# Routing without a stage of its own: choices and ranks inside the neighbouring stages, one memory region per expert

## The reference

```
x = x + layernorm(attention(layernorm(x)))     # 16 heads of 16, prefix-LM mask, output projection + bias
x = x + layernorm(moe(layernorm(x)))

def moe(x):                                     # 8192 tokens
    scores = softmax(x @ gate_w.T)              # 8 experts
    idx    = top_k(scores + gate_b, 2)
    cw     = one_hot(idx) * scores, summed      # weights of the two chosen experts
    y_e    = swiglu((x@w1_e.T + b1_e) * (x@w3_e.T + b3_e)) @ w2_e.T + b2_e
    return sum_e cw_e * y_e + shared expert(x)  # same form, for all tokens
```

## Time and profile before

| | us |
|---|---|
| median of 3 runs (2283.53 to 2286.15) | 2284.32 |
| profiled execution, its own time | 2304.21 |
| its span, first to last instruction | 2302.5 |

### The profile page before, as it was taken

One profiled execution on the slowest core, in us unless ns is written; L12 is line 12 of the kernel. 1 busy time (PEld: TensorE's weight loads), 2 busy tenths in 40 slices (PEclk: granted clock), 3 DMA queues, 4 the chain that ended last, 5 costly groups with the idle time before them and its releaser, 6 DMA issues. The chain is left out here.

```text
span 2302.5 us, 38058 instructions
## 1 busy us (share of the span) xinstructions
PE 2083.7 (90%) x14085; PEld 1272.9 (55%) x14085; DVE 1465.9 (64%) x2297; ACT 1698.6 (74%) x2162; POOL 661.2 (29%) x643
## 2 busy tenths in 40 slices
PE   7995999999999999999997883799999999999970
PEld 6782333333333333333333883688888888888860
DVE  5663255554555565554555895465688888888865
ACT  5664999999999999999996771333466666666645
POOL 1111000000000000000000450766335665666537
PEclk9997999999999999999999995899999999999995
DMA  6887645565544445555501771544467776677656
GB/s 222 309 289 182 131 90 97 105 104 102 102 65 89 88 87 93 104 105 73 86 10 51 233 267 65 188 161 163 161 199 213 193 173 176 171 186 187 174 168 252
DMA packets 162899, 340.50 MB, mean 148 GB/s; under 512 B 18048, under 2 KB 91904, under 8 KB 155424
## 3 DMA queue, kind: packets, MB, share of 16 engines
q1 hardware_dynamic: 130148, 284.29, 46.4%
q0 software_dynamic: 30256, 46.03, 10.7%
q10 hardware_dynamic: 2316, 7.80, 0.9%
HBM read 194.29 MB, written 143.62 MB: 147 GB/s over the span
## 5 line engine op out<-in xcount | busy, mean ns | idle before, releaser
L1114 ACT ACTIVATE att_prob<-att_scores 128x1024 f32<-128x1024 f32 (+2 forms) x1122 | 998.0, 1031 | 61.5 <-PE att_scores L1061 58.1
L1080 PE MATMUL att_out<-att_prob,att_va 128*32 128x512 f32 (+3 forms) x5000 | 578.9, 543 | 13.6 <-DVE att_prob L1146 12.1
L1061 PE MATMUL att_scores<-att_qs,att_ks 50*128 50x512 f32 (+3 forms) x2560 | 466.5, 431 | 22.9 <-PEq L116 17.2
L1061 PEld LDWEIGHTS att_scores<-att_qs,att_ks 50*128 50x128 f32 x2560 | 211.3, 185 | 495.4 <-ACT att_prob L1114 415.4
L1782 POOL DMA_INDIRECT sums<-moe_y,moe_token x142 | 307.1, 2162 | 247.9 <-ACT moe_y L2040 194.1
L1924 PE MATMUL moe_ps<-moe_xt_hi,moe_w_hi 128*128 128x512 f32 (+1 forms) x880 | 340.2, 387 | 21.5 <-ACT moe_h L2013 17.2
L1009 POOL DMA_DIRECT2D ctx_scr<-att_cout x64 | 55.1, 861 | 985.2 <-DVE att_cout L1196 946.2
L1924 PE MATMUL moe_ps<-moe_xt_hi,moe_w_lo 128*128 128x512 f32 (+1 forms) x880 | 333.8, 379 | 0.0
L1924 PE MATMUL moe_ps<-moe_xt_lo,moe_w_hi 128*128 128x512 f32 (+1 forms) x880 | 332.5, 378 | 0.0
L1146 DVE SCALAR_TENSOR_TENSOR att_prob<-att_prob,att_tri 128x512 f32<-128x512 f32 x224 | 144.8, 688 | 271.3 <-ACT att_prob L1114 271.3
L2013 ACT ACTIVATE moe_h<-moe_ps,moe_wb 128x512 f32<-128x512 f32 (+1 forms) x220 | 141.6, 650 | 112.6 <-PE moe_ps L1924 57.0
(11 more groups left out here) (259 smaller groups left out, 3201.9 us busy)
## 6 DMA issues: line engine op xcount, KB each, us to landing
qk_parts<-proj_qk SPq DMA_DIRECT2D x64, 512.0 KB, 4.6
keep_first_weights<-w_experts SPq DMA_DIRECT2D x22, 1412.0 KB
moe_wraw<-w_experts SPq DMA_DIRECT2D x21, 1412.0 KB
att_qs<-qk_parts SPq DMA_DIRECT2D x180, 128.0 KB
att_ks<-qk_parts SPq DMA_DIRECT2D x180, 128.0 KB
rows_in<-att_zeros SPq DMA_DIRECT2D x13, 1632.0 KB, 21.7
moe_rows<-rows_in SPq DMA_DIRECT2D x22, 544.0 KB
proj_xin<-x SPq DMA_DIRECT2D x16, 512.0 KB, 3.8
```

Source lines behind the costliest of these rows:

```text
L1061: last = nc.tensor.matmul(pss[e % SBUFS][:, h, at:at + CH - q0], ks[s][rows, half, kt * P:(kt + 1) * P], qs[s][rows, half, c * CH + q0:(c ...
L1080: last = nc.tensor.matmul(pso[k % 2][strip, q0:], va[team % 2][:, kt, strip], probs_of(u)[:, h, at:at + CH - q0], start=(kt == 0), stop=(i ...
L1114: nc.scalar.activation(probs_of(u)[:, half * 2:half * 2 + 2, start:], pss[e % SBUFS][:, :, start:], ACT.Exp, scale=HD ** -0.5)\
```

## The change

There is no routing stage. Each expert has a region of its own in `rows_in`, of 8192 + 512 rows, so that a token's place is `8704 * expert + rank` and needs no total counts. The 64 tiles are worked in 4 groups of 16:

- End of the output stage: the maximum is subtracted from the logits of groups 0, 1, 2 in steps 9, 13, 17 (group 3 behind the last step), with ScalarE's exponentials behind them. In steps 17 to 20 VectorE also makes shares and scores (17) and choices (18) of group 0, shares and scores of group 1 (19), ranks of group 0 and choices of group 1 (20). TensorE has two counting matmuls in step 18. The shared expert's weights are loaded at step 2 and cut into hi and lo in steps 17 and 18; the first rows are loaded at step 6.
- Inside `experts`: TensorE counts groups 1, 2, 3 behind block 0 of chunks 0, 2, 4 into the PSUM of the second product; VectorE makes their ranks at f = 1 of these chunks, shares and scores of groups 2, 3 at f = 3 of chunks 0, 2, their choices at f = 1 of chunks 1, 3. The tables of chunks follow at f = 1 and f = 3 of chunks 5, 6, 7. POOL waits for the ranks of a group ahead of chunks 4, 8 and 12.
- Filling: the zero fills during attention are gone (two transfers of 512 rows stay, one into `blank`). SP copies `blank` (512 rows, 557 KB) behind every expert's last row, 8 copies from memory to memory, ahead of its load of chunk 10.
- SP reads the start of each routed chunk from a table and loads from there.

```diff
+REGION = T + CH
+SPARE_AT = E * REGION
...
 # attention_out, SP
+                    if k == 2:
+                        sp.dma_start(first_raw[:], w_experts[E]).then_inc(w_loaded[0], 16)
+                    if k == ADD + 3:
+                        sp.wait_ge(xn_stored[0], 16)
+                        sp.dma_start(first_rows[:, :, 0:D], tok_ch[0]).then_inc(rows_loaded[0], 16)
...
 # attention_out, TensorE (CHOOSE_AT = CUT_AT = NCH + 1)
+                    if k == CHOOSE_AT + 1:
+                        count_first()
...
 # attention_out, ScalarE, at the end of a step
+                    if k == CUT_AT:
+                        act.wait_ge(w_loaded[0], 16)
+                        nc.scalar.activation(w_first[0][:, 0:W13], first_raw[:, 0:W13], ACT.Copy).then_inc(w_hi[0], 1)
+                    if k == CUT_AT + 1:
+                        nc.scalar.activation(w_first[0][:, W13:], first_raw[:, W13:WM], ACT.Copy).then_inc(w_hi[0], 1)
+                        nc.scalar.activation(wb_first[:], first_raw[:, WM:], ACT.Copy).then_inc(w_bias[0], 1)
...
 # attention_out, VectorE: behind residual, add_bias and context_lo of a step
+                    if k == CHOOSE_AT:
+                        shares_of(V, r, group_tiles(0), then)
+                        scores_of(V, r, group_tiles(0), then)
+                    if k == CHOOSE_AT + 1:
+                        best_two_of(V, r, group_tiles(0), tails, then)
+                        dve.sem_inc(marked, 1)
+                    if k == CHOOSE_AT + 2:
+                        shares_of(V, r, group_tiles(1), then)
+                        scores_of(V, r, group_tiles(1), then)
+                    if k == CHOOSE_AT + 3:
+                        dve.wait_ge(counted, 2)
+                        ranks_of(V, dve, r, 0, counts[:, 0], counts[:, 1], slot, then, counts_read, 0)
+                        best_two_of(V, r, group_tiles(1), tails, then)
+                    if k == CUT_AT:
+                        dve.wait_ge(w_hi[0], 1)
+                        V.tensor_tensor(w_first[1][:, 0:W13], first_raw[:, 0:W13], w_first[0][:, 0:W13].bitcast(F32),
+                                        ALU.subtract).then_inc(w_lo[0], 1)
...
+                shift_logits(GROUPS - 1)
...
+def ranks_of(V, dve, r, g, before, total, slot, then, counts_read, seen):
+    V.tensor_copy(r.total, total.rearrange("p (t e) -> p e t", e=E)).then_inc(counts_read, 1)
+    then(V.tensor_tensor_scan(r.upto..., r.keeps..., r.total..., 0.0, ALU.mult, ALU.add))
+    then(V.tensor_tensor(r.at, ... upto - total))
+    V.tensor_tensor(r.at, r.at, before..., ALU.add).then_inc(counts_read, 1)
+    then(V.tensor_tensor(r.at, r.at, bcast(r.run[g], 1, [P, GT, E]), ALU.add))
+    then(V.tensor_tensor(r.run[g + 1], r.run[g], r.upto[:, :, GT - 1], ALU.add))
+    then(V.tensor_tensor(r.tmp, r.hot[:, :, t], ..., ALU.mult))
+    then(V.tensor_reduce(r.slotf, r.tmp, AX_X, ALU.add))
+    then(V.tensor_copy(slot[:, :, t], r.slotf))
...
 # experts, SP
+        COUNT_AT, TABLE_AT, FILL_AT = (0, 2, 4), 5, 10
+                    if c == FILL_AT:
+                        sp.wait_ge(fills_known, 1)
+                        for e in range(E):
+                            at = sp.value_load(fill_at[0:1, e:e + 1], min_val=0, max_val=SPARE_AT)
+                            sp.dma_start(rows_in[bass.ds(at, CH), :]..., blank...).then_inc(blanked, 16)
...
+                            if k == 0:
+                                sp.wait_ge(blanked, E * 16)
+                                sp.wait_ge(experts_known, 2)
+                            at = sp.value_load(start_of[0:1, region(k):region(k) + 1], min_val=0, max_val=SPARE_AT)
+                            sp.dma_start(ring[b][:, 0:held], rows_in[bass.ds(at, held * P), :]...)
...
 # experts, TensorE
-                    hidden(n, s, range(0, FB - 1))
+                    hidden(n, s, range(0, 1))
+                    if c in COUNT_AT:
+                        count(COUNT_AT.index(c) + 1, c)
+                    hidden(n, s, range(1, FB - 1))
+                    if c - 1 in COUNT_AT or c in COUNT_AT[1:]:
+                        pe.wait_ge(counts_read, 2 * sum(1 for a in COUNT_AT if a <= c))
                     if prv is not None:
                         down(*prv)
...
 # experts, ScalarE, ahead of the first rows
+                        nc.scalar.activation(r.ex[:, t], r.ex[:, t], ACT.Exp).then_inc(r_exped, 1)
                         rows(0, 0)
-                        second_weights(0, 0)
...
 # experts, VectorE, behind u of block f and ahead of the rest
+                        route(c, f)
+                def route(c, f):
+                    if f == 1 and c in COUNT_AT:
+                        ranks(COUNT_AT.index(c) + 1)
+                    for g in range(2, GROUPS):
+                        if (c, f) == (COUNT_AT[g - 1] - 2, 3):
+                            shares_of(...); scores_of(...)
+                        if (c, f) == (COUNT_AT[g - 1] - 1, 1):
+                            best_two_of(V, r, t, tails, then)
+                            dve.sem_inc(marked, 1)
+                    # (5,1) halves, (5,3) bases, (6,1) singles, (6,3) owners, (7,1) places, (7,3) chosen
```

More of the change, by code:

```diff
@@ L920, in attend @@
         ZR = 12
[L921 to L922 removed]
+        assert len({(ZR * p + j) % CH for p in range(P) for j in range(TPC)}) == CH
         SR = (T + CH - FIRST * CH) // P // 2
@@ L1353, in router, with count_first @@
                     last.then_inc(g_done, 1)
+                def count_first():
+                    pe.wait_ge(marked, 1)
+                    both = r.both[:, group_tiles(0)].rearrange("p t e -> p (t e)")
+                    for i, left in enumerate((r.before, r.onesq)):
+                        nc.tensor.matmul(counts[:, i], left, both, start=True, stop=True).then_inc(counted, 1)
                 for k in range(STEPS):
@@ L1653, in experts @@
         HALVED = (3, PAIRS - 1)
-        whole = {p: ph.sb(f"acc{p}", [P, 2, TPC, D])[:] for p in range(3)}
+        places = [late[:, i * 2 * TPC * D:(i + 1) * 2 * TPC * D].rearrange("p (c j d) -> p c j d", c=2, j=TPC)
+                  for i in range(3 + EARLY)]
+        whole = {p: places[p] for p in range(3)}
         whole.update({4 + i: chunks_in(wraw[i][:], 2) for i in range(2)})
@@ L1942, in down, with count @@
                         last.then_inc(y_done[s], 1)
+                def count(g, c):
+                    if g > 1:
+                        pe.wait_ge(marked, g - 1)
+                        pe.wait_ge(y_biased[c % 2], c // 2 * 2)
+                    both = r.both[:, group_tiles(g)].rearrange("p t e -> p (t e)")
+                    for left, psum in ((r.before, psY[0]), (r.onesq, psY[1])):
+                        nc.tensor.matmul(psum[:, 0, 0:GT * E], left, both, start=True, stop=True).then_inc(counted, 1)
                 def step(n, s, nxt, prv):
+                    c = 2 * n + s
                     if prv is None:
@@ new lines, in owners @@
+                def owners():
+                    starts = r.chunk0.unsqueeze(2).broadcast_to(slots)
+                    then(V.tensor_tensor(r.past[:, :, 1:], starts, bcast(r.ends, 1, slots), ALU.is_ge))
+                    then(V.tensor_tensor(r.alone, starts, bcast(r.single, 1, slots), ALU.is_equal))
+                    then(V.tensor_tensor(r.alone, r.alone, bcast(r.odd, 1, slots), ALU.mult))
+                    then(V.tensor_tensor(r.mine, r.past[:, :, 0:E], r.past[:, :, 1:], ALU.subtract))
+                    then(V.tensor_tensor(own[:], r.mine, r.alone, ALU.add))
@@ new lines, in places @@
+                def places():
+                    starts = r.chunk0[0:1].unsqueeze(2).broadcast_to(one)
+                    then(V.tensor_tensor(r.from_[0:1], starts, bcast(r.shift[0:1], 1, one), ALU.add))
+                    then(V.tensor_tensor(r.from_[0:1], r.from_[0:1], r.mine[0:1], ALU.mult))
+                    then(V.tensor_tensor(r.also[0:1], r.alone[0:1], bcast(r.single_at[0:1], 1, one), ALU.mult))
+                    then(V.tensor_tensor(r.from_[0:1], r.from_[0:1], r.also[0:1], ALU.add))
+                    then(V.tensor_reduce(r.start[0:1], r.from_[0:1], AX_X, ALU.add))
+                    then(V.tensor_scalar(r.start[0:1], r.start[0:1], float(SPARE_AT), None, ALU.add))
+                    V.tensor_copy(start_of[:], r.start[0:1]).then_inc(experts_known, 1)
```

428 lines of the change are left out of this document (239 added, 189 removed).

## The result

| kernel | median us (runs) | against before, same chip | span of the profiled execution |
|---|---|---|---|
| before | 2283.93 (4) | | 2302.5 |
| changed | 2270.91 (4; 2269.0 to 2272.1) | 0.9937, 95% interval 0.9925 to 0.9950 | 2270.3 |

The change makes the kernel 13.0 us faster by the medians (0.57%; 0.63% by the paired ratio in the table), where 17.6 were forecast. The measured 2270.9 lies 4 us over the forecast's 2267 and inside its range of 2254 to 2282. The sum behind that has three parts: the start, the first chunks, and one that was not foreseen.

The account below looks back on a forecast made before the run. TensorE was taken to bound the experts, VectorE the output and routing stages. Start 27.6 gained, less 8.5 (chunks), 1.0 (counting) and 0.5 (contention), gave 17.6 us: 2267 from the median 2284.3, range 2254 to 2282.

Parts of the forecast that it names:

- the 1.3 of steps 9 and 13: Output stage: a maximum and a subtraction on 16 tiles in each of two steps, 4 x 0.33 = 1.3 us on VectorE.
- Tail and start: Output stage's end 9.1 us longer, routing stage gone, experts' weights already cut: first hidden matmul at 1417.3, 27.6 us gained.
- The chunks get heavier: First expert chunks: routing work beyond VectorE's 3.4 us spare, plus waits, costs 8.5 us, 3.5 of it in chunk 1.
- the forecast's upper bound: First expert chunks: 33 us lost if none of VectorE's added work fits in its spare time.
- Counting: TensorE in the first chunks: six counting matmuls of 128 columns, 0.8 to 3 us, taken as 1.0.
- Contention: Chunks while SP's blanking copies run: 0.5 us lost, load 10's landing otherwise hidden by rows held in the ring.
- an undisturbed chunk takes 14.62 us: Experts stage: TensorE's period from one set of transposes to the next, 1650.73 to 1665.35 in the kernel before.
- chunks from 9 on at 14.62: Sign expected in the trace after: expert chunks from 9 on keep 14.62 us.
- B: Rival, chance 0.22: VectorE's holes ahead of bias additions come through whole in the first eight chunks, 8 us more, 2275.
- C: Rival, chance 0.18: the hole of chunk 2, 12.0 us of TensorE behind ScalarE's wait, goes; 2255.
- D: Rival, chance 0.10: blanking copies are slow and hold back row loads; loss F - 35, at F of 59 time 2291.
- F: Time SP's eight blanking copies need: taken as 24 us; 59 by the zero fills' pace, about 46 by the HBM rule.

Follow-up runs that it names:

- e1: The kernel before, unchanged, measured and profiled a second time: 2284.02 us, span 2282.3.
- e4: Changed kernel with unused bytes added so that weights, rows xt and products ah lie modulo 128 bytes as in the kernel before: 2260.74 us, ratio 0.9895.
- e9: The kernel of e4 once more, unchanged, as control beside later runs: 2262.16 us, ratio 0.9906 to the kernel before.
- e10: On e4: first low weight cut behind last residual and choices, first count one step later, second group's choices ahead of first group's ranks: 2258.05 us, 0.9874.
- e12: On e4: 16 further copies of blank rows ahead of the 8 needed, same queue, three times the traffic: 2277.82 us, ratio 0.9972.
- e11: On e4: weight cut and first count later in the tail; second group's choices into chunk 0, countings, ranks, tables one chunk later: 2258.75 us, 0.9886.
- e3: Changed kernel with 96 bytes left free at SBUF's right end, so even chunks' weights begin on a multiple of 128 bytes: 2263.52 us, ratio 0.9913.
- e2: Kernel before with only the even chunks' weights moved, 96 bytes further in SBUF: 2291.19 us against 2283.81, ratio 1.0037.
- e7: On e4: rows xt moved 64 bytes down onto a multiple of 128 (u, gs, a, h3 moved too): 2274.19 us, ratio 0.9875.

## Why the prediction was right, and where it was not

**Where the 13 us are.** Compared hole-free, changed kernel against e1: from chunk 14's residual to the first hidden matmul 38.3 against 67.7 us (29.4 gained); from there to the end 853.9 (2270.3 - 1416.4) against 839.9 (2282.3 - 1442.4), 14.0 lost; and the residual itself is at 1378.1 against 1374.7, 3.4 later. 29.4 - 14.0 - 3.4 = 12.0, the difference of the two spans; the medians say 13.0. Starts of that residual differ by up to 3 us between profiles of one kernel (1378.7 in e4, 1376.0 in e9), so of the 3.4 hardly more than the 1.3 of steps 9 and 13 can be put down to the change.

**Tail and start: right, step by step.** VectorE free for the last residual at 1390.4 (forecast 1389.9), choices done 1397.7 (1397.4), router 1407.3 (1407.2), experts' first transposes 1410.4 (1411.1), first hidden matmul 28.5 us earlier (27.6). Operations on 128x128 are 0.29 long and 0.33 apart, as bounded. What the forecast took as given, e10 took away: reordering alone gives 5.3 of these us back.

**The chunks get heavier: right mechanism, size too large.** "8.5 in all" by VectorE, 1.0 for counting and 0.5 for contention made 10.0. (The pieces listed for chunks 0 to 7 add up to 31.9 us of VectorE's time, not 33; only the forecast's upper bound rests on it.) Measured in e4, where nothing else differs in pace: 0.51, 0.65, 1.41, 0.12, 1.15, 0, 0, 1.01, together 4.85 over 14.62 each. The 3.5 forecast for chunk 1 was 0.65: the waits that I followed were there (0.74, 0.34, 0.35 us), but shorter. Counting: six matmuls in three pairs, each pair 0.36 to the next start and 0.09 of the next one's; 1.35 us, forecast 1.0. Contention: in e4 the copies run beside chunks 5 and 6, which lose nothing, forecast 0.5. TensorE's own count and one of the waits, in e4:

```profile
1480.89 0.60 PE L2011 MATMUL moe_psY<-late 128*128 128x128 f32 x4
...
1479.39 0.50 PE L1985 MATMUL moe_ps<-moe_xt_hi,w_first_hi 128*128 128x512 f32 x1 [0.35 <-DVE moe_u L2321]
```

Chunk 7's loss is not the copies: it follows on owners(), five operations of 0.5 us ahead of the limit of u at the end of chunk 6, which reach TensorE through ScalarE (0.72 us for `moe_h`). With three times the copies it is the same 15.64.

**What failed: a term that was not in the sum.** The step that failed is "an undisturbed chunk takes 14.62 us", taken over unasked, and with it "chunks from 9 on at 14.62". The change moves `w_first` and `late` to the right end of SBUF and shifts the rest by what it adds and frees. e4 differs from the changed kernel in unused bytes alone: from the first hidden matmul to the end it takes 845.3 instead of 853.9 us, and the medians are 8.8 (e9) and 10.2 us (e4) lower. The account from the forecast to the spans: 17.6, + 0.5 (the start from the residual on: 29.4 against 27.6 + 1.3), + 5.15 (chunks: 4.85 for 10.0), - 8.6 (pace), - 0.55 (unassigned, later in the experts), - 2.1 (ahead of the tail, within the spread of profiles) = 12.0. That the time came out only 4 us off is in part luck: two errors of opposite sign met; without the one of pace the forecast would have been 5 to 6 us too high.

**Rivals.** B and C both took the holes as the program's; e1 and e9 show kernels without them, and the changed kernel's profile has none. Neither had a case to decide. D fell on its input, not on its rule. The copies' DMA share, changed kernel:

```profile
1505.00:1515.00 10.00, 10.00 (x49) 8.19 (x48) 6.90 (x14) 3.82 (x5) 7.28 (x8) 1.00 0.95 349
1515.00:1525.00 10.00, 10.00 (x61) 8.76 (x60) 7.19 (x16) 2.33 (x3) 7.05 (x8) 1.00 1.02 384
```

They are issued from 1501.5 on, and the eighth, issued at 1511, lands 10.1 us later; so F, the time that the copies need, was some 20 us, forecast 24. The first row load behind them lands about 1524, 31 us into chunk 5, forecast 35. Issues of the changed kernel from 1510.9 to 1511.5, and from 1511.8 to 1511.9 (KB, us from issue to landing):

```profile
rows_in<-blank SPq DMA_DIRECT2D x1, 544.0 KB, 10.1
```

```profile
moe_rows<-tokens SPq DMA_DIRECT2D x1, 512.0 KB, 12.4
```

The zero fills' pace (59) was the wrong row. From the figure of about 358 GB/s of HBM per core in the Trainium skill, "DMA: Bandwidth & Descriptors", Specifications, the forecast estimated 46 us for F. The trace doesn't agree: F was 20, and all traffic ran at 384 GB/s over 10 us. That rate counts a copied byte once: the 16 further copies of e12 raise the total of the packets from 324.4 to 333.3 MB, and both HBM read and HBM written by the same 8.9.

**The best version** is e10: 2258.05 us, 26.0 under the kernel before beside it, and 12.9 under the change as made, which was measured on another occasion. e11 is not told apart from it.

## What to carry to other kernels

A change that allots or frees memory moves the operands of matmuls it never touches; ask for the addresses of weights and moving operands modulo 128 bytes before and after, and put the padding back before judging the idea: here 96 and 64 unused bytes were worth 9 to 10 us, where the whole change had gained 13. Where work is moved into another stage, price the order of the queue and not only the work: e10 is faster by 4 us with not one operation fewer. And take a second profile of the kernel before when the profiled execution is not at its median.

## What the runs showed of the hardware that was not expected

- With `xt` on a multiple of 128 bytes and the weights 96 bytes past one, 128x512 matmuls took 401, 396 and 396 ns (changed kernel); with both on one, 395, 390 and 389 (e3); with the weights on one and `xt` 64 past, 398, 393 and 392 (e4). There was no idle time and the clock was at its upper level. One pair of weights moved by 96 bytes in the kernel before cost 7.4 us of 2284 (e2).
- Output matmuls (128x256) took 278 ns in e4 and 281 in the changed kernel, but also 280 or 281 in e7, where neither of their operands had moved against e4. Where the pace comes from is thus not known beyond the sets of places tried.
- While copies from memory to memory ran, the core's whole traffic was 349 to 384 GB/s (a copied byte counted once) with DMA shares of 0.95 to 1.02, and TensorE stayed busy throughout. Eight copies of 557 KB took some 20 us, 24 of them 49 to 50.
- Stretches of 1 to 12 us in which several engines wait for nothing that the profile shows appeared in all profiles of one comparison, in which the kernel before took 2301.8 us, in the first profile of the kernel before, and in none of two other comparisons, one of them on the same chip.
